# Attention and experts kernel: output projection in three rounded products, by halves of a block

## The reference

```python
x = x + attention(layernorm(x), Wq, Wk, Wv, Wo, betas)
x = x + ffn(layernorm(x))
# attention: 16 heads, DK = DV = 128, a scan over 32 segments of 64 tokens
att_mem = sigma_q @ mem / (sigma_q @ z);  att_dot = softmax(causal scores) @ vv
delta = vv - sigma_k @ mem / (sigma_k @ z)
mem_new = mem + sigma_k^T @ delta
att = beta * att_mem + (1.0 - beta) * att_dot          # (B, H, SEG, DV)
out = att.reshape(Bsz, SEG, H * DV) @ Wo               # no transposition of heads
# ffn: gate with 32 experts in 4 groups, best 2 groups, then best 4 experts,
# each expert keeps its first CAP = 64 tokens; plus a shared expert
```

## Time and profile before

| what | value |
|---|---|
| time, median of 3 runs (lowest to highest) | 1655.94 us (1655.25 to 1658.43) |
| the profiled execution's own time | 1656.93 us |
| its span, first to last instruction | 1655.1 us |
| PE busy | 1626.1 us |
| DVE, ACT, POOL busy | 1138.9, 884.3, 495.9 us |
| mean granted TensorE clock | 0.997 |

### The profile page before, as it was taken

One profiled execution on the slowest core, in us unless ns is written; L12 is line 12 of the kernel. 1 busy time (PEld: TensorE's weight loads), 2 busy tenths in 40 slices (PEclk: granted clock), 3 DMA queues, 4 the chain that ended last, 5 costly groups with the idle time before them and its releaser, 6 DMA issues.

```text
span 1655.1 us, 42788 instructions
## 1 busy us (share of the span) xinstructions
PE 1626.1 (98%) x17260; PEld 1421.5 (86%) x17260; DVE 1138.9 (69%) x3509; ACT 884.3 (53%) x1955; POOL 495.9 (30%) x438
## 2 busy tenths in 40 slices
PE   8899999999999999999999999999999999999898
PEld 7798999899998999898999989898999989986555
DVE  7865857585775757575776758575876767589544
ACT  6564646465563646365664646364654646462131
POOL 2332323232332313331333313231333323230361
PEclk9999999999999999999999999999999999999999
DMA  6102121211102121312112020312112020327957
GB/s 208 27 21 78 40 73 33 81 33 55 58 29 84 36 72 34 86 34 58 49 35 85 29 78 28 86 34 65 42 41 78 29 78 23 95 90 214 315 103 216
DMA packets 121781, 122.07 MB, mean 74 GB/s; under 512 B 24032, under 2 KB 101296, under 8 KB 121456
## 3 DMA queue, kind: packets, MB, share of 16 engines
q1 hardware_dynamic: 118224, 113.52, 23.0%
q0 software_dynamic: 3328, 5.81, 1.8%
q10 hardware_dynamic: 32, 0.01, 0.0%
HBM read 94.90 MB, written 24.40 MB: 72 GB/s over the span
## 4 chain that ended last, share of the span: by engine, by line
PE 92%; DVE 5%; DMA 1%; issue 1%; ACT 0%; POOL 0%; SPq 0%; DVEq 0%; POOLq 0%; ACTq 0%
PE bank_p L1502 23%; PE bank_v L1620 13%; PE chain_k L1575 6%; PE chain_k L1553 6%; PE bank_a L1510 5%; PE bank_v L1510 5%; PE chain_q L1553 5%; PE bank_s L1523 4%; PE bank_a L1591 3%; PE chain L1553 3%; PE bank_p L1533 3%; PE bank_a L1602 2%; PE bank_v L1602 2%; PE bank_s L1608 2%; PE chain L1575 2%; PE bank_p L1683 1%
## 5 line engine op out<-in xcount | busy, mean ns | idle before, releaser
L595 POOL TENSOR_TENSOR step_place<-step_place 128x512 f32<-128x512 f32 x128 | 166.0, 1297 | 574.9 <-ACT step_place L741 426.3
L763 ACT ACTIVATE step_place<-chain_q,step_place 128x128 f32<-128x128 f32 x384 | 112.8, 367 | 221.1 <-DVE step_place L999 221.1
L1620 PE MATMUL bank_v<-step_place 128*128 128x256 f32 x1024 | 225.3, 381 | 0.7 <-ACT step_place L774 0.7
L1502 PE MATMUL bank_p<-xt_hi,w_hi 128*128 128x256 f32 x1024 | 220.0, 296 | 3.0 <-DVE step_place L987 2.9
L1620 PEld LDWEIGHTS bank_v<-step_place 128*128 128x128 f32 x1024 | 193.2, 190 | 29.2 <-issue 2.6
L1502 PE MATMUL bank_p<-xt_hi,w_lo 128*128 128x256 f32 x1024 | 206.4, 283 | 0.0
L1502 PE MATMUL bank_p<-xt_lo,w_hi 128*128 128x256 f32 x1024 | 206.3, 283 | 0.0
L632 POOL TENSOR_TENSOR step_place<-step_place 128x512 f32<-128x512 f32 x64 | 69.3, 1082 | 435.4 <-DVE step_place L1267 435.4
L1502 PEld LDWEIGHTS bank_p<-xt_hi,w_hi 128*128 128x128 f32 x1024 | 158.3, 191 | 22.4 <-issue 13.8
L987 DVE SCALAR_TENSOR_TENSOR step_place<-step_place,bank_p 128x512 f32<-128x512 f32 x128 | 87.4, 684 | 107.6 <-ACT bank_p L735 107.6
L1502 PEld LDWEIGHTS bank_p<-xt_hi,w_lo 128*128 128x128 f32 x1024 | 159.8, 192 | 0.0
(11 more groups left out here) (225 smaller groups left out, 3959.9 us busy)
## 6 DMA issues: line engine op xcount, KB each, us to landing
step_place<-in_L_attn_Wo_dram SPq DMA_DIRECT2D x128, 256.0 KB, 2.8
step_place<-beta_all SPq DMA_DIRECT2D x64, 256.0 KB, 3.3
expert_place<-in_L_ffn_w_dram SPq DMA_DIRECT2D x24, 512.0 KB, 8.2
expert_sums<-zero SPq DMA_DIRECT2D x16, 272.0 KB, 5.2
expert_rows<-rows_place SPq DMA_DIRECT2D x15, 288.0 KB, 2.3
step_place<-in_L_attn_x_dram SPq DMA_DIRECT2D x16, 256.0 KB, 3.9
turned<-in_L_attn_x_dram SPq DMA_DIRECT2D x16, 256.0 KB, 3.9
x_rows<-rows_place SPq DMA_DIRECT2D x16, 256.0 KB, 2.9
```

The source lines that it names most:

```text
L595: nc.gpsimd.tensor_tensor(dl[seg][:, :, 0:DK], val[:, seg, :, :], beta_rows[:, :, :], ALU.mult).then_inc(s["vb_ready"], 1)
L763: ins = nc.scalar.activation(to[:, j, :], t[:, at:at + DK], ACT.Copy, scale=rd[:, seg, r:r + 1])
L1502: ins = mm(out, w[:, g, m, c, col], x[:, c, :, :].rearrange("p s t -> p (s t)"), start=i == 0, stop=i == len(parts) - 1)
L1620: ins = mm(bank_v[:, b * D:(b + 1) * D], att[:, b * PIECES + i, :], wo[:, i % WR, :], start=(i == 0 and b == 0), stop=(i == PIECES - 1), s ...
```

## The change

The output projection is made per half block, of three `fp32r` products, in 128 slots. A half is the 128 rows that two groups of heads give. A slot is a quarter of a half's projection: 4 pieces of `Wo`, 12 matmuls of 128 x 256. In step n, slot 2n-5 stands between the two halves of the projection of k, and slot 2n-4 behind the last numerators. The slots 123 to 127 stand behind the loop, between pieces of the shared expert.

- `Wo` is split into high and low parts at the start: 4 loads of 512 KB, four copies by ACT (`wo_high`), four subtractions by POOL (`wo_low`), four stores of 1 MB to the scratch `wo`. POOL then loads 1 MB for every slot into one buffer (`load_wo`), 128 times.
- ACT writes the high parts of the attended columns. DVE takes the low parts straight from the banks (`attended_low`, two of 128 x 512 per step).
- DVE adds every slot's result to the residual's rows in SBUF (`out_add`, 128 x 256, two per step) in place of `residual`. PE waits for it (`out_added`) before `project_v(1)` and before the second attended transposes.
- The rows of a half lie in another order over the partitions. So the residual is loaded, and the routing rows stored, by 8 transfers of 16 partitions each; at the end the sums are loaded by 32 transfers in place of 8, and the output stored by 64 on SP with 8 more on SP and 8 on ACT in place of 12.
- The groups come in the order 0, 1, 3, 2. The statistics of x1 move to g = 2, its transposes and logits to g = 3, and a block's gate into the next block; the gate of block 15 comes behind the loop. The rounds on `mid` are split 3 and 5 around block 16's gate, with a width of 384 in place of 256.

```diff
-        def project_out(blk, n):
-            pe.wait_ge(s["att_ready"], 2 * n)
-            for i in range(PIECES):
...
-                for b in range(B):
-                    ins = mm(bank_v[:, b * D:(b + 1) * D], att[:, b * PIECES + i, :],
-                             wo[:, i % WR, :], start=(i == 0 and b == 0), stop=(i == PIECES - 1),
...
+        def project_out(k, bank=bank_v, start=True, stop=True):
+            half, quarter = divmod(k, QS)
+            g = slice(half % 2, half % 2 + 2)
+            if quarter == 0:
+                pe.wait_ge(s["att_split"], 4 * (half + 1))
+            pe.wait_ge(wo_arrived, 16 * (k + 1))
+            for i in range(WR):
+                a = quarter * WR + i
+                for which, (x, w) in enumerate(((att_hi, 0), (att_hi, 1), (att_lo, 0))):
+                    ins = mm(bank[:, 0:D], x[:, a, g, :].rearrange("p g m -> p (g m)"), wo[:, i, w, :],
...
+            ins.then_inc(s["wo_used"], 1)
...
+        def load_wo(k):
+            if k:
+                pool.wait_ge(s["wo_used"], k)
+            else:
+                pool.wait_ge(s["wo_moved"], 32 * QS)
+            pool.dma_start(wo[:, :, :, :], scratch["wo"][:, k % QS * WR:(k % QS + 1) * WR, :, :]
+                           ).then_inc(wo_arrived, 16)
...
+        def out_add(k, bank=bank_v):
+            half = k // QS
+            dve.wait_ge(s["wo_used"], k + 1)
...
+            rows = x_half[half % 3]
+            nc.vector.tensor_tensor(rows, rows, bank[:, 0:D], ALU.add).then_inc(s["out_added"], 1)
+        def attended_low(n):
+            for seg in range(2):
+                dve.wait_ge(s["att_ready"], 2 * n + seg + 1)
+                hi, lo = att_parts(n, seg)
+                nc.vector.tensor_tensor(lo, seg_bank[seg][:, :].rearrange("p (b a m) -> p b a m", b=B, a=PIECES),
+                                        hi.bitcast(fp32), ALU.subtract).then_inc(s["att_split"], 1)
...
+        def wo_high(c):
+            act.wait_ge(s["wo_moved"], 16 * QS)
+            if c:
+                act.wait_ge(s["wo_split"], 2 * c)
+            if c >= 2:
+                act.wait_ge(s["wo_moved"], 16 * (QS + 2))
...
+        for k in range(SLOTS - QS, SLOTS):
+            load_wo(k)
```

More of the change, by code:

```diff
@@ L395, in body @@
             else:
-                for c in range(WR // WC, H // WC):
-                    load_wo(blk, c)
-                for c in range(WR // WC):
-                    load_wo(blk + 1, c)
-                store_x1(blk)
+                if not last:
+                    load_x(blk + 1)
+                load_res(2 * blk)
                 zero_part(blk)
             load_betas(n + 2)
-            if not first:
-                store_columns(blk)
             if last:
@@ L822, in body @@
                     split_hi(g + 2, 2)
-                if g == 1 and not first:
+                if g == 3 and not first:
                     side_x1t(blk)
@@ L1290, in body @@
                     split_lo(g + 2, 2)
-                if g == 0 and not first:
-                    residual(blk)
-                    x1_stats(blk)
-                    x1_newton(blk, 0, 1)
                 if g == 1 and not last:
@@ L1309, in body, with gate @@
                     state(n, g, 1)
+        def gate(blk):
+            gate_scores(blk)
+            gate_group_sums(blk)
+            gate_groups(blk)
+            gate_best(blk)
+            gate_top(blk)
+            gate_picks(blk)
+            gate_weights(blk)
         blocks(dve, body)
         attended(NT - 1)
+        out_add(SLOTS - QS - 1, bank_o)
+        attended_low(NT - 1)
+        gate(NBLK - 1)
+        shared_mul(0, 0)
         earliest(ROUNDS + 1)
@@ L1319, in _ @@
         ins.then_inc(s["lists_kept"], 1)
-        shared_mul(0, 0)
-        dve.wait_ge(s["pickv_ready"], NBLK)
-        dve.wait_ge(s["lists_kept"], 1)
-        for r in range(MID_FIRST):
-            top8(mid_kept, mid, r)
-        residual(NBLK)
+        picks(NBLK - 1)
+        shared_mul(0, 1)
+        dve.wait_ge(s["wo_used"], SLOTS)
+        dve.wait_ge(s["xres_arrived"], 128 * 2 * NBLK)
+        rows = x_half[(2 * NBLK - 1) % 3]
+        nc.vector.tensor_tensor(rows, rows, bank_v[:, 0:D], ALU.add).then_inc(s["out_added"], 1)
         x1_stats(NBLK)
@@ L1652, in _ @@
         pe.wait_ge(s["x_normed"], 1)
[L1653 removed]
+        x_transposes(bank_v)
         pe.wait_ge(s["gw_arrived"], 16)
@@ L1805, in body @@
                     x_transposes()
+                if g == 3 and not first:
+                    x1_transposes(blk)
+                if n >= 2:
+                    project_out(2 * n - 4)
+                if g == 2 and not last:
+                    pe.wait_ge(s["x_turned"], blk + 1)
+                if g == 3 and not first:
+                    pe.wait_ge(s["x1t_ready"], blk)
                 if nxt:
```

501 lines of the change are left out of this document (298 added, 203 removed).

## The result

The changed kernel takes 1717.86 us (median of 4 runs, 1715.02 to 1719.14) against 1656.26 before: a ratio of 1.0368, interval 1.035 to 1.0386. It is 61.6 us slower by the two medians. (The 1656.26 is of the 3 runs of the table before and one more.) Slower was forecast, by 32, so the sum had half of it; the wide range, 1645 to 1740, held the time, A's own range did not. The traced execution took 1719.14.

A forecast was written before the change was run, and what follows sets the result against it. PE's own work was taken to bound the loop. The terms summed as 1655.1 - 30.6 + 19 + 8 + 24 + 12 = 1687.5, corrected by + 1.8 - 1.0 to 1688 us, range 1645 to 1740.

The forecast's parts named there:

- A: Whole kernel: the main forecast, all five terms summed to 1688 us, own range 1665 to 1705, chance 0.57.
- Term 1: Loop: fifteen projections of 14.01 us leave PE and 123 slots of 1.46 come in, -30.6 us.
- Term 2: Loop: PE waits for DVE's `out_add`, 12 us in steps g = 0 and 7 in g = 2, +19 us.
- Term 3: Start: ACT's copies and POOL's subtractions of `Wo` wait for the first stores and delay the path, +8 us.
- Term 4: Tail: five slots alternate with 5.9 us loads in one buffer, +19, and four more `mid` rounds, +5; together +24 us.
- Term 5: End: SP issues 104 small loads and stores at 0.40 us each in place of 20 transfers, +12 us.
- B: Loop and tail: `Wo` arrives late in the loop as well, giving 1725 us, chance 0.20.
- C: Loop: slots fill gaps PE already has and cost less than 1.46 us, for example 1628 us; chance 0.15.
- D: Whole kernel: no change, `out_add` stalls fall away and tail and end cost half, about 1655 us, chance 0.08.

The follow-up runs named there:

- Run 10: Changed kernel with DVE's `x1_apply` placed ahead of the two `attended_low` in steps with g = 3: 1707.69 us, ratio 1.0301.
- Run 3: Changed kernel with batch 1's last loads and stores issued by ACT, batch 0's by SP, all still over 16 partitions: 1712.14 us, ratio 1.0339.
- run 4: Changed kernel with the sums loaded by 32 transfers of 128 KB, each over 128 partitions in place of 16, stores unchanged: 1707.89 us, ratio 1.0306.
- run 2: Changed kernel with the 32 loads of the sums made 8 over all partitions, the small stores kept: 1705.66 us, ratio 1.0294.
- run 11: Changed kernel with natural row order and wide end, two more tail buffers for `Wo`, later `Wo` split, and `x1_apply` ahead of `attended_low`: 1656.25 us, ratio 0.9995.

## Why the prediction was right, and where its sizes were off

**Term 1, PE's work, -30.6.** Right. Less its waits (0.66 and 0.33) the block takes 90.28, 2.32 less than before; that is one projection of 14.01 out and eight slots of 1.46 in. PE's busy time in the loop's stretch fell by 30.2. The run with two products gave 58.8 where 59.0 were worked out from 0.12 us a matmul, on runs that tell some 4 us.

**Term 2, DVE late, +19.** Near in its sum and wrong in its place, so its nearness is luck. The waits that came into the loop are 9.2 for `x1_apply`, 3.9 for `out_add`, 1.7 for `Wo` and some 2 more, and PE's idle time there rose by 13.9. I put 0.85 into the wait for `out_add` in g = 0; it is 0.33, in 12 steps. The terms that I added give 9.04 and not 9.1, and so 0.78. DVE came to the add another 0.56 earlier than worked out: statistics and delta take 0.33 less than my 3.38, which held a wait of 0.24 for PE's numerators (ahead of 772.10) that is not there now, and the group sums take 0.99 in place of 1.24. I put 7 into g = 2, where there is nothing, and nothing into g = 3, where 9.2 stand. There I had counted what DVE loses, and had not looked at what comes in: before, `x1_apply` and the transposes behind it stood in step g = 1, and the trace has no wait of PE for it; in g = 3 it stands behind the two new subtractions of 0.60 each, and PE comes to it 0.66 us too early. Run 10 took this wait away by order alone. The waits of a moved step are to be worked out in the step that it moves to.

**Term 3, the start, +8.** The mechanism as described, the size 14.3, above its bound of 12. I had let half of copies and subtractions run beside the wait; ACT takes them in turn, wait, copy, wait for POOL, copy, 10.5 us, and everything of step 1 stands behind. I had named the waits of the third and fourth copy alone; by the trace the second cost 3.4. And I had no term for the clock, 1 us.

**Term 4, the tail, +24.** 27.3 + 5.9 = 33.2. A load of 1 MB took 5.3 in the median, and from the start of its issue to the slot 5.1 to 5.5, where I had 5.9: over the first four loads of the tail this is 2.3 less. Three things made the stretch longer by 8.4 all the same. The last load ran beside the experts' weights, 8.7 us: +2.8. PE starved, its granted clock fell (0.83 from 1510 to 1530, where PE is busy half of the time), and a slot that takes 1.65 to its last end at the full clock took 2.2 once and 2.9 three times: +5.2 over the five against my 1.5, of which 4.4 over the 1.65. And slot 122 ended 3.1 us after the numerators in place of 1.5, behind transposes that wait for `x1_apply`: +1.6. The rest, about 1, is the 0.3 to 0.5 us between a slot's end and the next issue, which I had left out. The four rounds more on `mid` and the wider lists came out near, 5.9 for 5. For the rate the Trainium skill's section "Anatomy of one DMA — SWDGE (gpsimd) path" of "DMA: Bandwidth & Descriptors" would give 4.4 us, an estimate; the trace's 128 loads lie above it, 5.0 to 9.4 us with a median of 5.3.

**Term 5, the end, +12.** The step that failed by most: 29.2. I priced the issue, and took the landing of a small transfer as that of any other. SP did issue almost without a break, as I had written, but at 0.64 us a load and 0.52 a store (20.34 / 32 and 33.26 / 64) in place of 0.40, and the loads' issue was not the limit. Run 3 halves the time to issue them and the third add comes as late; run 4 keeps their number and size, makes them wide, and the adds come as early as with 8. So the narrow form makes the sums land in 36.9 us (4.19 MB, 114 GB/s over the whole). The other part of the term, the issue of the stores behind the last adds, is near what I had: 0.47 each where the loads are wide (run 2). By the runs the loads' form is worth 12 and that of the stores 17. The Trainium skill has the parts of an explanation in "DMA: Bandwidth & Descriptors": section "Where 436 GB/s comes from" counts 16 ports into the on-chip memory, and section "The descriptor swizzle" shows each port serving partitions in runs of four. By an estimate from the first section's 435 GB/s, a transfer over 16 neighbouring partitions would so use 4 ports of 16, and have 109 GB/s. The trace's 121 GB/s, held from 1660 to 1692, are near it and a tenth above, so the estimate does not fit as it stands. No run here varied the width between 16 and 128, and none kept the stretches in memory the same, so the ports as cause are argued and not shown.

**The rivals.** B did not come: the loop's loads took 5.3 in the median and two steps in 62 waited for one, 0.86 and 0.82 us; the other five waits for `Wo` stand in the tail. C was refuted by the two products. D did not come: run 11 is where it put the time, but there edits had taken the losses out. Its own sum has a slip: half of the end's 12 is 6 and not 10, which gives 1650.5. The sum was right in sign because its losses in start, tail and end had places of their own in the trace and none came out smaller than forecast; it was low by 30 us, 17 of them in the end, 6 in the start, 9 in the tail, 2 between, less 5 in the loop.

## What to carry to other kernels

A faster product in the loop pays only what is left after its supplies: here 30 us of matmul time were bought with 14 us of waits in the loop and with 78 us of start, tail and end. Where a change alters the order of rows over partitions, follow it to the last loads and stores: nothing hides them there, and there the transfers over 16 partitions landed as slowly from two queues as from one. Put the awkward order where a loop covers it. A single buffer whose load takes 5 us cost 1.7 us in all between 123 uses 8 us and more apart, and all of it behind the loop, where the uses follow at once; and the price of a moved vector operation is read in the step where it comes to stand.

## What the runs showed of the hardware that was not expected

- The same 128 KB in pieces of 1 KB land in 2.9 us over 128 partitions and in 7.4 over 16, and in 18 where two queues issue the narrow form (medians; the narrow form also reads from eight places in memory in place of one). The DMA engines' busy share is 0.97 at 305 GB/s in the wide form and 1.11 at 126 in the narrow one, so it does not tell how much they move.
- Narrow stores of 16 KB and pieces of 64 bytes in the loop, 67000 packets more, cost no time that the runs can tell (29.0 us faster with them, 29.5 without).
- Where PE starves for some microseconds at a time, at the start, in the tail and at the end, its granted clock falls: to a mean of 0.50 from 55 to 60 us, after a wait of 10 us; to 0.83 from 1510 to 1530, where PE is busy 10.0 of 20 us; to 0.84 over the loads of the sums, busy 26.1 of 36.9. Matmuls of 256 columns then start 0.21 apart in place of 0.12 (1499.04 to 1499.46 for two of them). So idle time there costs more than itself: 4.4 us over the five slots of the tail, against 1.65 a slot at the full clock.
